# Normalisation on ScalarE, C turned after the projection, the batch change of the scan spread out, and a scatter from columns: one change to a kernel of a state-space layer and a mixture of experts

## The reference

```python
def _layernorm(x, axis=-1, eps=1e-05):
    m = jnp.mean(x, axis=axis, keepdims=True)
    v = jnp.var(x, axis=axis, keepdims=True)
    return (x - m) / jnp.sqrt(v + eps)
...
    dt = soft_clamp(softplus(einsum('bld,ed->ble', x, W_dt) + b_dt), 0.001, 0.1, 0.5)
    Bp = einsum('bld,nd->bln', x, W_B)
    Cp = einsum('bld,nd->bln', x, W_C)
    A = -exp(soft_clamp(A_log, -5.0, 5.0, 0.5))

    def step(h, inp):
        t, x_t, dt_t, B_t, C_t = inp
        dA = exp(soft_clamp(dt_t[:, :, None] * A[None], -8.0, 8.0, 0.5))
        h = h * dA + (dt_t * x_t)[:, :, None] * B_t[:, None, :]
        hnorm = sqrt(sum(h ** 2, axis=(1, 2), keepdims=True))
        scale = minimum(20.0 / (hnorm + 1e-08), 1.0)
        h = where(t % 10 == 0, h * scale, h)
        y = einsum('bdn,bn->bd', h, C_t) + D_param * x_t
        return (h, y)
...
    logits = xt @ gate_w.T
    topk_w, topk_idx = top_k(softmax(logits, axis=-1), 3)
...
x = x + _L0_attn_ref(_layernorm(x), ...)
x = x + _L0_ffn_ref(_layernorm(x), ...)
```

## Time and profile before

| | |
|---|---|
| median of three runs | 1890.44 us (1887.22 to 1893.2) |
| the profiled execution | 1890.26 us, span 1888.5 us |
| mean granted clock of TensorE, of full speed | 0.879 |
| busy share: PE, DVE, ACT, POOL | 80%, 60%, 41%, 62% |
| first stage, 161.3 us: PE, DVE, ACT, POOL busy | 121.1, 113.4, 82.0, 96.3 us |
| scan, 474.0 us: PE, DVE, ACT, POOL busy | 302.5, 428.9, 361.5, 404.1 us |
| scatter, 312.7 us: PE, DVE, ACT, POOL busy | 226.6, 71.7, 38.9, 216.4 us |

### The profile page before, as it was taken

How to read it: one execution, slowest core, us unless ns; L and a number is a source line. 1 busy time by engine, 2 the same in 40 slices (tenths; PEclk the granted TensorE clock), 3 DMA queues, 4 the chain that set the end, 5 groups by cost and what they waited for, 6 DMA issues and landing times. The chain is left out here.

```text
span 1888.5 us, 25364 instructions
## 1 busy us (share of the span) xinstructions
PE 1504.3 (80%) x5738; PEld 934.9 (50%) x5738; DVE 1126.0 (60%) x2125; ACT 772.4 (41%) x1284; POOL 1164.7 (62%) x1181
## 2 busy tenths in 40 slices
PE   5883667666666596399997089999999999995997
PEld 2332444444434495255555056666666666663555
DVE  7783999999999586522224034444444444442598
ACT  3556878787778111111110033333433333332210
POOL 5676988889889231467568556666666666663000
PEclk9996887888889655699999589999999999998999
DMA  4323233332232361566751022222222222224895
GB/s 149 121 96 111 79 112 123 112 123 90 101 122 90 124 200 58 141 148 150 161 103 45 3 76 88 88 88 87 87 87 90 87 87 89 87 87 147 304 333 212
DMA packets 138087, 221.21 MB, mean 117 GB/s; under 512 B 21021, under 2 KB 103173, under 8 KB 137989
## 3 DMA queue, kind: packets, MB, share of 16 engines
q1 hardware_dynamic: 100053, 138.17, 22.6%
q0 software_dynamic: 27840, 60.96, 10.2%
q10 hardware_dynamic: 10096, 20.86, 5.0%
HBM read 153.13 MB, written 66.79 MB: 116 GB/s over the span
## 5 line engine op out<-in xcount | busy, mean ns | idle before, releaser
L1686 PE MATMUL bank<-arena_dt,xgT 128*128 x832 | 394.2, 596 | 0.1
L735 PE MATMUL bank<-ident,state 128*128 128x128 f32 x1024 | 192.2, 325 | 169.6 <-DVE state L792 63.6
L711 POOL TENSOR_TENSOR state<-arena_x,b_all 128x1024 f32<-128x1024 f32 x128 | 298.6, 2354 | 40.0 <-DMA b_all<-bc_rows 27.1
L1645 POOL DMA_INDIRECT choice_out<-ye,ids x208 | 204.6, 984 | 165.2 <-DVE ye L1785 161.8
L792 DVE TENSOR_TENSOR_SCAN state<-bank,state 128x1024 f32<-128x1024 f32 x128 | 291.7, 2279 | 21.2 <-POOL state L711 21.1
L1771 DVE TENSOR_TENSOR hid<-bank,arena_x 128x512 f32<-128x512 f32 x208 | 143.9, 692 | 251.0 <-PE bank L1686 251.0
L1636 POOL DMA_INDIRECT xg<-x_norm,tokens x208 | 200.5, 964 | 84.9 <-issue 61.0
L735 PEld LDWEIGHTS bank<-ident,state 128*128 128x128 f32 x1024 | 134.8, 165 | 231.2 <-DVE state L792 157.2
L1523 POOL DMA_INDIRECT row_choice<-choice,to_row x192 | 194.6, 1014 | 56.6 <-issue 51.4
L1703 PE MATMUL bank<-arena_x,gluT 128*128 x832 | 213.9, 380 | 0.0
L1751 ACT ACTIVATE gluT<-bank 128x256 f32<-128x256 f32 x208 | 79.7, 383 | 322.8 <-PE bank L1695 321.3
(11 more groups left out here) (158 smaller groups left out, 2186.4 us busy)
## 6 DMA issues: line engine op xcount, KB each, us to landing
b_all<-bc_rows SPq DMA_DIRECT2D x64, 512.0 KB, 3.6
arena_x<-choice_out SPq DMA_DIRECT2D x64, 384.0 KB, 7.6
xin<-in_x SPq DMA_DIRECT2D x16, 512.0 KB, 4.0
x_skip<-xin SPq DMA_DIRECT2D x16, 512.0 KB, 3.0
y_acc<-x_skip SPq DMA_DIRECT2D x8, 1024.0 KB, 5.7
x_mid<-y_acc SPq DMA_DIRECT2D x8, 1024.0 KB, 4.5
x<-x_mid SPq DMA_DIRECT2D x16, 512.0 KB, 4.6
x_norm<-xnb SPq DMA_DIRECT2D x16, 512.0 KB, 3.2
```

The costliest lines, as they stand in the source:

```text
L711: pool.tensor_tensor(state[j % STATES][:, :, here], gT[:, :, b, here], b_all[j % 2][:, here].unsqueeze(1).to_broadcast([P, KD, TH]), ALU.m ...
L735: last = pe.transpose(bank[:, TURN + (BY_PE * j + q) % 2, i * D + k * P:i * D + (k + 1) * P], state[j % STATES][:, k, t * P:(t + 1) * P], ...
L1645: pool.indirect_dma_start(out=choice_out, out_offset=bass.IndirectOffsetOnAxis(ap=ids[:, j % 2, j // 2:j // 2 + 1], axis=0), in_=ye[c][:], ...
L1686: last = pe.matmul(bank[:, 2 + s, :], xgT[s][:, k, :], w1[:, k, ds(e_no * (2 * F), 2 * F)], start=(k == 0), stop=(k == KD - 1))
```

## The change

*First stage.* `normalise` moves from DVE to ACT as an activation Identity with scale `rstd` and bias `off` = -mean * rstd, four for a group, each of 256 elements; it stands one group ahead of `copy_xT` in ACT's stream. POOL makes `minus_mean` and `off` (two small operations more) and makes the inverse deviations one group earlier. DVE measures two groups ahead, not one. PE turns C behind the projection, not ahead of it. `bc` has four buffers.

*Scan.* `make_dt` moves from DVE to ACT (Identity with a scale and the offset `dt_mid`), for the first batch ahead of the first tanh, for the others at n = 4 behind a clamp at n = 3; `times_dt` follows at n = 6 and 7; that of the first batch is split between DVE and POOL. The square moves from POOL to ACT (206 elements of every tenth time step), with two buffers `sq_one`; POOL only adds. `b_all` has three buffers; SP stores a finished batch at n = 6 and loads at n = 0. DVE's `check` and `take_sum` stand behind the unit's second scan.

*Scatter.* The copies go; the indirect DMAs take a column of the wide tiles, written out without a loop, and each tile's wait is for the DMAs of four tiles back.

```diff
@@ first stage @@
+            bc = [sb(f"bc{c}", [2 * N, CH]) for c in range(4)]
...
+                        pool.tensor_scalar(minus_mean[s][:], meanvar[s][:, :, 0], -1.0, None, ALU.mult)\
+                            .then_inc(mean_turned, 1)
                         pool.tensor_tensor(rstd[s][:], rstd[s][:], minus_half[:].to_broadcast([P, GT]), ALU.pow)\
                             .then_inc(rstd_made, 1)
...
+                        pool.tensor_tensor(off[s][:], minus_mean[s][:], rstd[s][:], ALU.mult).then_inc(off_made, 1)
...
-                            last = dve.tensor_scalar(xn[s][:, i, :], xin[c][:, i, :], meanvar[s][:, i, 0:1],
-                                                     rstd[s][:, i:i + 1], ALU.subtract, ALU.mult)
...
+                        act.wait_ge(x_loaded[c], (g - c) * 4 + 16)
+                        act.wait_ge(off_made, g + 1)
+                        wait(act, xn_turned, g - 1)
+                        wait(act, dx_made, g - 1)
+                        for i in range(GT):
+                            last = act.activation(xn[s][:, i, :], xin[c][:, i, :], ACT.Identity, bias=off[s][:, i:i + 1],
+                                                  scale=rstd[s][:, i:i + 1])
...
@@ scan @@
+                        act.activation(dtT4[:, :, b, :], dtT4[:, :, b, :], ACT.Identity, bias=dt_mid[:, 0:1],
+                                       scale=DT_HALF / SHARP).then_inc(dt_made, 1)
...
+                    def square(j):
...
+                        act.activation(onto[:], state[j % STATES][:, :, 0:T:SEG], ACT.Square).then_inc(sq_taken, 1)
...
+                        square(j)
-                        if n == 1 and b + 1 < NB:
+                        if n == 3 and b + 1 < NB:
                             clamp_dt(b + 1)
+                        if n == 4 and b + 1 < NB:
+                            make_dt(b + 1)
...
-                        if n in (4, 6) and b + 1 < NB:
-                            times_dt(b + 1, (n - 4) // 2)
+                        if n in (6, 7) and b + 1 < NB:
+                            times_dt(b + 1, n - 6)
...
-                        wait(sp, u_made, 2 * (j - 1))
+                        wait(sp, u_made, 2 * (j - BUFS + 1))
...
@@ scatter @@
-                    def copy_rows(it, c, t):
-                        wait(pool, c_sent[c], 48 * it)
-                        pool.tensor_copy(to_row[c][:], row_i[:, ds(t, 1), :].rearrange("p o k -> p (o k)"))
...
+                    for t in range(TILES):
+                        c = t % 4
+                        wait(pool, c_sent[c], 48 * (t // 4))
                         for k in range(TOPK):
                             pool.indirect_dma_start(
-                                out=row_choice, out_offset=bass.IndirectOffsetOnAxis(ap=to_row[c][:, k:k + 1], axis=0),
-                                in_=choice[c][:, k:k + 1], in_offset=None).then_inc(c_sent[c], 16)
+                                out=row_choice, out_offset=bass.IndirectOffsetOnAxis(ap=row_i[:, t, k:k + 1], axis=0),
+                                in_=choice_all[:, t, k:k + 1], in_offset=None).then_inc(c_sent[c], 16)
```

More of the change, by code:

```diff
@@ L319, in model_kernel @@
             rstd = [sb(f"rstd{s}", [P, GT]) for s in range(2)]
+            minus_mean = [sb(f"minus_mean{s}", [P, GT]) for s in range(2)]
+            off = [sb(f"off{s}", [P, GT]) for s in range(2)]
             mag = [sb(f"mag{s}", [P, KD, CH]) for s in range(2)]
[L321 to L322 removed]
+            bc = [sb(f"bc{c}", [2 * N, CH]) for c in range(4)]
+            bc_kept, bc_sent = sem("bc_kept"), sems("bc_sent", 4)
+            mean_turned, off_made = sem("mean_turned"), sem("off_made")
             c_loaded = sem("c_loaded")
@@ L365, in _ @@
                     for j in range(GROUPS - 4, GROUPS):
-                        store_bc(j, j % 2)
-                    for s in range(2):
-                        sp.wait_ge(bc_sent[s], 8 * GROUPS)
+                        store_bc(j, j % 4)
+                    for c in range(4):
+                        sp.wait_ge(bc_sent[c], 4 * GROUPS)
                 @block.gpsimd
@@ L597, in model_kernel @@
             state = [sb(f"state{s}", [P, KD, T]) for s in range(STATES)]
-            b_all = [sb(f"b_all{s}", [P, T]) for s in range(2)]
+            BUFS = 3
+            b_all = [sb(f"b_all{s}", [P, T]) for s in range(BUFS)]
             sq = [sb(f"state_sq{s}", [P, KD, NORMS]) for s in range(2)]
-            sq_one = sb("sq_one", [P, KD, NORMS])
+            sq_one = [sb(f"sq_one{s}", [P, KD, NORMS]) for s in range(2)]
             scaled = [sb(f"scaled{s}", [P, 3 * D]) for s in range(2)]
@@ L820, in _ @@
                             add_y(j - 1, 1)
+                        scan(j, 1)
+                        if j > 0:
+                            add_y(j - 1, 4)
                         if n == 1 and b > 0:
@@ L853, in load_b @@
                         b, n = j // N, j % N
-                        wait(sp, u_made, 2 * (j - 1))
-                        sp.dma_start(b_all[j % 2][:], bc_rows[n, b * T:(b + 1) * T].partition_broadcast(P))\
-                          .then_inc(b_loaded[j % 2], 16)
-                    load_b(0)
-                    load_b(1)
+                        wait(sp, u_made, 2 * (j - BUFS + 1))
+                        sp.dma_start(b_all[j % BUFS][:], bc_rows[n, b * T:(b + 1) * T].partition_broadcast(P))\
+                          .then_inc(b_loaded[j % BUFS], 16)
+                    for j in range(BUFS):
+                        load_b(j)
                     load(0)
                     load(1)
-                    for j in range(2, UNITS + 1):
+                    for j in range(BUFS, UNITS + 1):
                         if j < UNITS:
                             load_b(j)
-                        b = (j - 3) // N - 1
-                        if (j - 3) % N == 0 and b >= 0:
-                            store(b)
-                            if b + 2 < NB:
-                                load(b + 2)
+                        if j % N == 6 and j > N:
+                            store(j // N - 1)
+                        if j % N == 0 and N < j < UNITS:
+                            load(j // N)
                     store(NB - 1)
```

144 lines of the change are left out of this document (66 added, 78 removed).

## The result

The change makes the kernel faster: 1833.56 us (median of four runs, 1826.84 to 1849.06) against 1889.8 (1887.22 to 1893.2), a ratio of 0.9713 (95% interval 0.965 to 0.9776). The forecast was 1822, in a range of 1800 to 1850. The profiled execution, 1849.06 us with a span of 1847.4, is the slowest of the four.

A forecast was written before the change was run, and what follows sets the result against it. Stages run behind barriers, each bound by its last engine: DVE stretching the first stage and pacing the scan, POOL holding the scatter. From 1890.3 us, -14 (first stage), -11 (scan) and -43 (scatter) gave 1822, range 1800 to 1850.

The forecast's parts named there:

- First stage, -14: Normalise, project, softplus: normalisation on ScalarE brings groups from 8.45 to 7.4 us, the first 1.5 later; bounds -22 to 0.
- The loop that the forecast put at 7.4: First stage: dependencies closing over three groups through ScalarE, POOL, row store, load and DVE; 21.7 us, with semaphore hops 7.4 a group.
- Scan, start, -1.8: Before the first scan: dt to ScalarE costs 0.5 us, one of POOL's two products moved to DVE saves 2.3.
- Scan, the rest: After the scan's start: DVE's dt -10.2 us, POOL's later waits -11.5, ScalarE's added work +12.6.
- a forecast of 12.6: Scan: with square and dt, ScalarE makes DVE late by 3.1 instead of 1.3 us a batch, over seven batches.
- Scatter, -43: Scatter stage: copies and most landing waits go, POOL still ends it, next stage at 1040 instead of 1083.6; bounds -50 to -19.
- so most vanish; I keep 4: Scatter: waiting four tiles back instead of three cuts POOL's 27.9 us of waits for landings to 4.
- all else was over near 1034: Scatter: SP idle 49.2 us at the barrier was taken to mean that POOL alone holds the stage after 1034.
- forecast's own signs of being wrong: Groups of 8 us or more, square far over 0.4, many landing waits, or a scatter stage ending on another engine.
- The landings set the scatter: Rival: DMA engines deliver at their own rate, POOL waits as long, 24 us stay; 1846 us, chance 0.12.
- ScalarE becomes the bound: Rival: first-stage groups take 8.4 us, the scan loses in waits what it gains, only scatter gains; 1847 us, chance 0.13.
- the strided square: Rival, slower: ScalarE's square above 0.9 us lengthens each of 64 scan units; at 2.35 us, 1903 us; chance 0.04.

The follow-up runs named there:

- norm_first: The change with the normalisation alone back on DVE, at the head of DVE's step; first stage 159.1 us, groups 8.32 us apart.
- square_on_pool: The change with the square alone back on POOL; scan 461.8 us.
- late_scatter: The change, but POOL begins the 192 indirect DMAs only when the shared expert has added nine of its ten groups; 2036.94 us.
- eight_back: The change with the shared expert's rows loaded two groups ahead and POOL's scatter wait eight tiles back instead of four; 1840.4 us, ratio 0.9698.
- dt_on_pool: As eight_back, with the second half of dt for the seven later batches on POOL instead of ScalarE; 1827.41 us, ratio 0.9632 to the kernel before.
- dt_on_dve: The change with the second half of dt alone back on DVE, a unit after the clamp; scan 484.1 us.
- scatter_alone: The kernel before with only the scatter of the change; 1863.26 us against 1895.63, ratio 0.9841.

## Why the prediction was right, and where it was wrong

The forecast was right in its sign and within 12 us; two stages came out near their terms, and the third at half to three quarters of its own. The result lies in the range because that reached up to the rivals at 1846 and 1847; the profiled execution, 1849.06, is at its edge.

- *First stage, -14, measured -12.6: right.* Four normalisations on ScalarE took 2.07 us (2.2 forecast), a group 7.58 (7.4), the first came 1.43 later (1.5). norm_first shows that the normalisation on DVE, beside POOL, makes DVE hold the stage at 8.32; that this was the cause of the 8.45 too is argued, since there DVE was busy for 84.9 of 100 us and PE also waited for C. The loop that the forecast put at 7.4 was not taken apart. DVE's product, for which the forecast kept the old price, now meets POOL and took 2.13 us on the mean instead of 1.23, POOL's first small operation 0.77 instead of 0.24, and the 0.2 us for hops between engines stands on no row. The Trainium skill's rule that additions and multiplications belong on VectorE ("ScalarE: Activation LUTs", "Rules for kernel authors") would have made this stage longer; the measurement decides against it here, since ScalarE's 2.07 stands against DVE's 3.41, not 1.38.
- *Scan, start, -1.8, measured -0.5* (first scan 13.7 us after the stage's start, 14.3 before): the step took 2.33 us for DVE's product, and beside POOL's it took 3.40; and the first dt had taken DVE 1.23 us, not the mean of 1.46, so ScalarE's 2.00 added 0.8 and not 0.5.
- *Scan, the rest: right in sum, -12 over all runs for -11.* POOL's 11.5 us of later waits went. dt left DVE as said. The waits for transposes grew by 16.2 in the profiled execution, by some 10 in the others (23.0 to 26.6 us; 12.8 to 16.5 with the scan of before), for a forecast of 12.6. They stand where the forecast had them: the pairs behind clamp and dt are 2.8 to 3.1 us a batch, for 3.1. A square took 0.57 us, not 0.37; square_on_pool bears out that it is a part of these pairs (1.3 to 1.9 us a batch without it), though the scan was no shorter. The waits of 0.2 to 4.0 us in other units, the longest of them in a stretch at a granted clock of 0.50, are in no term.
- *Scatter, -43, measured -22 here, and -22 to -31 in the seven runs with this scatter and no other edit in that stage (281.3 to 290.6 us, median 284.1).* The copies went as forecast, and the issues took 188.9 + 55.1 = 244 us for 252. That was luck: the few long issues that the forecast kept went because POOL was done before DVE's pair came. Two steps failed. The landings, "so most vanish; I keep 4": 16.7 us stayed, beside a landing of 9.0 us instead of 7.0. And "all else was over near 1034": the shared expert's end was taken as fixed, but the transfers it lives on are slowed by the very DMAs that were packed closer. late_scatter and eight_back show it from both sides (229 us without them; POOL free of waits, and a stage of 284.4 us all the same, 276.8 in dt_on_pool). Two of the forecast's own signs of being wrong thus came: landing waits that stay, and a scatter stage that ends on another engine.
- *The rivals.* "The landings set the scatter" (1846) named half of it. "ScalarE becomes the bound" and "the strided square" did not come: 0.57 us stays under the 0.89 that ScalarE had idle.

Of the 15.5 us between the profiled execution and the median, the traces show about 4 in the scan (the last unit at a granted clock of 0.50) and 6 in the scatter, each against the median of its runs; the rest is open.

## What to carry to other kernels

When one engine's stream holds a stage and the rest idles at the barrier, the gain from shortening it is not simply that idle time: ask what the same work, packed closer, does to the transfers on which the others live, and take their end as a term that moves. A move to another engine is judged by how long the instruction takes at its place beside its neighbours: DVE's 1.35 us were 3.41 beside POOL, so ScalarE's steady 2.07 won. And before a buffer is added, look at what stands in front of the load in its queue. A total of waits can also stand still while its parts move, as in square_on_pool: look at where they stand before a cause is struck out.

## What had not been expected of the hardware

The same DVE instruction takes its plain time or over twice that, depending on POOL: four normalisations 1.35 or 3.41 us, dt 1.22 or 3.14, a product of 128x1024 1.23 or 3.40, while the scans (2276 to 2279 ns on the mean) and the additions from PSUM (468 to 471 ns) stay the same in every kernel. In the scan of the change the product of 3.40 us began with POOL's of 2.35 and ended 1.08 us after it, and in dt_on_dve the dt of 3.14 at 425.38 too ended 1.08 us after POOL's instruction beside it: so most of DVE's work stood behind POOL's end.

```profile
154.14 3.40 DVE L814 TENSOR_TENSOR arena_x<-arena_x,arena_dt 128x1024 f32<-128x1024 f32 x1 [5.20 <-ACT arena_dt L654]
```
```profile
154.11 2.35 POOL L722 TENSOR_TENSOR arena_x<-arena_x,arena_dt 128x1024 f32<-128x1024 f32 x1 [6.39 <-ACT arena_dt L654]
```

The Trainium skill, "SBUF — State Buffer", "Who interferes with whom", gives a rule for it: a DVE instruction in a mode that uses both ports, or one with two SBUF inputs beside a GpSimd instruction that reads SBUF, contends with GpSimd for a shared port pair, and the one that comes second "fully blocks". The trace agrees for these three, and for the ones that read PSUM, which do not change. That page infers that a DVE product of two SBUF inputs does not hold up GpSimd in making a DMA's descriptors; in the five kernels where POOL issued DMAs beside such a pair, those issues took 3.5 to 4.3 us (4.26 and 3.76 in scatter_alone, where the four ahead of them took 0.96), so here the measurement differs.

192 DMAs of 128 values each, 2% of the DMA engines' time themselves, made the other transfers of the stage take 191 us of engine time instead of 104, and landed in 9.0 us themselves instead of 3.4. Which part of the path they share was not tried.
